# Two attentions and two FFNs on Trainium2: the last eight query groups of the second attention run behind its first steps, and its query tiles come in another order

## The reference

```python
x = x + attn_a(layernorm(x))   # differential attention, 8 heads of 2 x 64, full softmax
x = x + ffn(layernorm(x))      # one 1024 x 1024 matrix rounded to int4, bias, rank-16 LoRA
x = x + attn_b(layernorm(x))   # causal attention, 16 heads of 64, rotary q and k
x = x + ffn(layernorm(x))      # the same weights again
```

```python
q, k, v = split((x @ W_qkv))             # 16 heads of 64 each
q, k = rope(q), rope(k)
att = q @ k.T / sqrt(64) + causal mask
y = softmax(att) @ v
return y @ W_o
```

## Time and profile before

| what | value |
|---|---|
| median of 3 runs | 1709.23 us (1708.33 to 1766.12) |
| the profiled execution, its own time | 1708.93 us |
| its span on the page, slowest core | 1706.1 us (1699.2 to 1706.4 us over the cores) |
| span of core 3, whose trace is read here | 1706.4 us |
| TensorE (PE) busy | 1497.0 us, 88% |
| ScalarE (ACT) busy | 1268.7 us, 74% |
| VectorE (DVE) busy | 1047.3 us, 61% |
| GpSimd (POOL) busy | 532.5 us, 31% |
| mean granted TensorE clock, core 3 | 0.966 |

### The profile page before, as it was taken

One profiled execution on the slowest core, in us unless ns is written; L12 is line 12 of the kernel. 1 busy time (PEld: TensorE's weight loads), 2 busy tenths in 40 slices (PEclk: granted clock), 3 DMA queues, 4 the chain that ended last, 5 costly groups with the idle time before them and its releaser, 6 DMA issues.

```text
span 1706.1 us, 40220 instructions; the slowest of 8 cores (1699.2 to 1706.4 us)
## 1 busy us (share of the span) xinstructions
PE 1497.0 (88%) x13132; PEld 787.9 (46%) x13344; DVE 1047.3 (61%) x1939; ACT 1268.7 (74%) x1904; POOL 532.5 (31%) x1089
## 2 busy tenths in 40 slices
PE   3899978789999999999999998759998899989987
PEld 1344434455555555555555555324443344444443
DVE  4474468878788787888878788432625454324215
ACT  2666649899999999999999999103234688878990
POOL 3010014444444444554444444522623000001001
PEclk9899989999999999999999999879997799989989
DMA  9614031211101111111111222473005222222303
GB/s 183 120 56 110 35 77 56 82 31 32 56 19 41 41 31 51 18 44 39 32 49 45 68 31 56 78 116 81 1 1 97 40 81 69 66 72 41 101 7 77
DMA packets 131468, 99.54 MB, mean 58 GB/s; under 512 B 99891, under 2 KB 115379, under 8 KB 131270
## 3 DMA queue, kind: packets, MB, share of 16 engines
q1 hardware_dynamic: 113910, 82.10, 18.0%
q0 software_dynamic: 17360, 14.88, 6.4%
HBM read 67.79 MB, written 20.97 MB: 52 GB/s over the span
## 4 chain that ended last, share of the span: by engine, by line
PE 41%; ACT 25%; issue 12%; DVE 5%; DMA 2%; POOL 0%; ACTq 0%; DVEq 0%; SPq 0%; POOLq 0%
ACT E L175 13%; PE pL L164 10%; ACT Gt L175 7%; PE pBb L164 6%; PE pY L171 5%; ACT EB L175 4%; PE pB L164 4%; PE pS L166 4%; PE pYb L171 4%; PE pL L166 3%; PE pD L164 3%; DVE Sx L184 2%; PE pS L164 1%; DMA xn<-xn 1%; PE pY L164 1%
## 5 line engine op out<-in xcount | busy, mean ns | idle before, releaser
L184 DVE TENSOR_TENSOR Sx<-pL,Gt 128x512 f32<-128x512 f32 x768 | 503.2, 685 | 138.3 <-PE pL L963 53.9
L175 ACT ACTIVATE E<-Sx 128x1024 bf16<-128x1024 f32 (+1 forms) x512 | 433.1, 846 | 15.4 <-DVE Sx L184 14.9
L175 ACT ACTIVATE EB<-pS,cst 128x1024 bf16<-128x1024 f32 (+1 forms) x320 | 296.5, 988 | 66.6 <-PE pS L166 63.7
L171 PE MATMUL pY<-V,E 128*128 128x129 bf16 x4096 | 308.2, 221 | 23.9 <-ACT E L175 11.7
L175 ACT ACTIVATE Gt<-pD 128x512 bf16<-128x512 f32 x512 | 306.4, 598 | 24.4 <-PE pD L164 15.4
L171 PEld LDWEIGHTS pY<-V,E 128*128 128x128 bf16 x4096 | 259.7, 98 | 92.7 <-issue 40.3
L166 PE MATMUL pL<-Q,K 64*128 64x256 bf16 x1536 | 198.8, 274 | 23.8 <-ACT E L175 15.8
L164 PE MATMUL pD<-Qn,K 128*128 128x256 bf16 x1024 | 196.4, 273 | 23.1 <-ACT Gt L175 15.8
L189 POOL TENSOR_SCALAR st<-st 128x1 f32<-128x1 f32 x64 | 17.8, 278 | 502.9 <-DVE st L439 486.3
L175 ACT ACTIVATE E<-pL 128x512 bf16<-128x512 f32 x256 | 154.1, 602 | 6.0 <-PE pL L171 0.5
L166 PE MATMUL pS<-Q,K 64*128 64x512 bf16 (+3 forms) x640 | 123.4, 379 | 21.8 <-ACT EB L175 15.7
(11 more groups left out here) (165 smaller groups left out, 2167.8 us busy)
## 6 DMA issues: line engine op xcount, KB each, us to landing
x<-xN SPq DMA_DIRECT2D x32, 512.0 KB, 5.2
x<-x SPq DMA_DIRECT2D x32, 512.0 KB, 3.3
out<-x SPq DMA_DIRECT2D x16, 512.0 KB, 2.8
x<-fker SPq DMA_DIRECT2D x3, 2048.0 KB
x<-WoT SPq DMA_DIRECT2D x2, 2048.0 KB
xn<-xn SPq DMA_DIRECT2D x16, 256.0 KB, 2.1
w_k<-WkT POOLq DMA_DIRECT2D x2, 1024.0 KB, 40.7
w_v<-WvT POOLq DMA_DIRECT2D x2, 1024.0 KB, 58.2
```

The costliest lines, as they stand in the source:

```text
L171: q.add(lambda e: e.matmul(out, lhsT, rhs, start=first, stop=last, skip_group_check=True))
L175: q.add(lambda e: e.activation(out, in_, func, **kw))
L184: q.add(lambda e: e.tensor_tensor(out, a, b, op))
```

## The change

- **Query groups.** The eight Q groups of tile 2 leave stage three and become a generator `last_q`. Its first 8 matmuls (all of head pair 0) are issued ahead of the attention; the rest is the first generator of the background. It uses `pY[0]` as its only bank and `pY[1]` for the permuted product. When it ends it frees `Wo`, starts the load of `WoB` and the load of the third block of `x`.
- **No barrier.** `phase_barrier` goes. The first score waits for GpSimd's last rope addition of the first pair of tiles, the first exponential for the last matmul of stage three's groups. The PSUM banks of stages three and four are now the same tensors: `pS` are `pL`, the three Y banks are `pD`, `pB` and `pY[1]`. As `pY[1]` is in use until `last_q` is over, the first eight units use the banks 0 and 1 only; after them the three go round.
- **Order of tiles.** 1, 0, 2, then the first 256 queries of tile 3, then the last 256. A step of a half tile takes two key blocks by 256 queries (four score matmuls of 256 columns, one exponential unless it is the unit's last step, which has two). Units are 8, 4, 12, 7 and 8 steps long, 312 steps in all, and a half tile's unit needs one Y bank.
- **Background.** `after_b` takes a range of blocks (4, 4, 4, 2, 2). It is added 6 steps after the tile's last unit, and `ffn` of a block starts at the earliest 4 steps after its transpose was issued (`lag`).

The core of the diff:

```diff
-    pL = [ps(f"pL{i}", p2) for i in range(4)]
+    pS = [p2.enter_context(nc.psum_tensor(f"pL{i}", [128, 2, QT], F32)) for i in range(2)]
+    pL = [pS[i // 2][:, i % 2, :] for i in range(4)]
...
         sy.wait(a_tok, xT_free.get(slot))
+        xT_clock[b] = bg.clock + state["lag"]
...
-        while b not in xT_tok:
+        while b not in xT_tok or bg.clock < xT_clock[b]:
             yield 0
...
-        for t in reversed(two):
+        for t in reversed(two) if pair == 0 else two[1:]:
             for h in range(HA):
                 group_q(t, h)
-        while late:
-            late.pop(0)()
-    phase_barrier()
-    p2.close()
+        if pair == 0:
+            while late:
+                late.pop(0)()
+            rope_tok = po.done()
+            x_free[0] = x_free[1] = ve.done()
+    w3_dead = pe.done()
+
+    def last_q(t):
+        nonlocal w_bank
+        for h in range(HA):
+            i = h % 2
+            pe.wait(w_bank, w_tok[h // 4], xs_tok[t])
+            for c in range(NCH):
+                mm(pe, pY[0][:, :], Wo[:, c, 128 * h:128 * (h + 1)], xs[t][:, c, :],
+                   c == 0, c == NCH - 1)
+                yield 1
+            p_tok = pe.done()
+            yield 0
+            ac.wait(p_tok, qb_free[i])
+            act(ac, qb[i][:, :], pY[0][:, :], AF.Copy)
+            b_tok = ac.done()
+            yield 0
+            pe.wait(b_tok, pss_free[1])
+            mm(pe, pY[1][:, :], perm[:, :], qb[i][:, :], True, True)
+            qb_free[i] = pe.done()
+            ve.wait(b_tok, t_free[i], cs_tok[t])
+            tt(ve, t1[i][:, :], pY[0][:, :], x[:, t, 0:QT], OP.mult)
+            w_bank = ve.done()
+            ve.wait(qb_free[i])
+            tt(ve, t2[i][:, :], pY[1][:, :], x[:, t, QT:2 * QT], OP.mult)
+            pss_free[1] = ve.done()
+            po.wait(pss_free[1])
+            tt(po, Q[:, h, QT * t:QT * (t + 1)], t1[i][:, :], t2[i][:, :], OP.add)
+            t_free[i] = po.done()
+            yield 0
...
+        po.wait(p_tok)
+        for hf in range(2):
+            state["WoB"] = sl_w[0].start(po, Wo[:, :, 512 * hf:512 * (hf + 1)],
+                                         w_cols(di["WoB"], 512 * hf, 512))
...
+    w_bank = pss_free[0]
+    pair1_q = last_q(2)
+    for _ in range(NCH):
+        next(pair1_q)
+    while late:
+        late.pop(0)()
...
-    pYb = [ps(f"pYb{i}", p4) for i in range(3)]
+    y_banks = [pD, pB, pY[1]]
+    ac.wait(w3_dead)
+    state["lag"] = 4
+    groups = [(QT, QT), (0, QT), (2 * QT, QT), (3 * QT, QA), (3 * QT + QA, QA)]
...
+            for p in range(last + 1):
+                steps.append((q0, nq, c, len(bank_of), [n * p + k for k in range(n)], p == last))
...
+        pe.wait(E_tok.get(s - 2), rope_tok if s == 0 else None)
+        if s < 2:
+            pe.wait(*pqk_free[2 * s:2 * s + 2])
+        if q0 == 2 * QT:
+            pe.wait(state["rope"])
...
     def y_bank(i, k):
-        return (2 * i + k) % 3
+        return k if i < HB // 2 else (bank_of[i] + k) % 3
...
         if c == HB // 2 - 1:
-            bg.add(after_b(t, [yn_tok[v] for v in range(i - c, i + 1)]))
+            toks = [yn_tok[v] for v in range(i - c, i + 1)]
+            bg.later(6, lambda: bg.add(after_b(q0, nq, toks)))
+
+    bg.gens.append(pair1_q)
```

More of the change, by code:

```diff
@@ L929, in build_program @@
     state["ln3"] = True
+    state["lag"] = 0
+    xT_clock = {}
     bg = Background()
@@ L1293, in build_program, with after_b @@
     rb = [sb(f"rb{i}", (128, 8), F32, s4) for i in range(2)]
-    p4 = contextlib.ExitStack()
-    pS = [p4.enter_context(nc.psum_tensor(f"pS{i}", [128, 2, QT], F32)) for i in range(2)]
-    pYb = [ps(f"pYb{i}", p4) for i in range(3)]
-    pB = ps("pBb", p4)
-    state["banks"] = Banks([pB[:, :]])
+    y_banks = [pD, pB, pY[1]]
+    y_free = [x_free[0], x_free[0], None]
+    ac.wait(w3_dead)
     state["ln3"] = False
-    for hf in range(2):
-        wo_tok = sl_w[0].start(po, Wo[:, :, 512 * hf:512 * (hf + 1)],
-                               w_cols(di["WoB"], 512 * hf, 512))
+    state["lag"] = 4
     out_tok = [None] * NTB
-    x_free = [None] * 4
-    xm_free = [None] * 4
+    xm_free = [w3_dead] * 4
     xT_tok.clear()
     xT_free.clear()
-    for b in range(4):
+    groups = [(QT, QT), (0, QT), (2 * QT, QT), (3 * QT, QA), (3 * QT + QA, QA)]
+    t_order = [q0 // 128 + i for q0, nq in groups for i in range(nq // 128)]
+    for b in t_order[:2] + t_order[3:4]:
         load_x(d_x2, b)
[L1312 to L1316, removed]
+    def after_b(q0, nq, y_toks):
+        bs = range(q0 // 128, (q0 + nq) // 128)
+        for b in bs:
+            yield from out_proj(b, y_toks, state["WoB"], False)
             layer_norm(b, ve, b % 4, lambda a_tok, b=b: turn_ln(b, b % 4, a_tok, b % 4))
-        for b in four:
+        for b in bs:
             yield from ffn(b, b % 4)
@@ L1321, in after_b, with key_blocks @@
             out_tok[b] = x_free[b % 4] = r_st.next(sy).start(sy, rows_of(d_out, b), x[:, b % 4, :])
[L1322 to L1326, removed]
-        for c in range(HB // 2):
-            for j in range(4 * t + 4):
-                blocks.append((t, c, j))
-    NB = len(blocks)
+            for v in t_order[t_order.index(b) + 4:][:1]:
+                load_x(d_x2, v)
+    steps = []
+    bank_of = []
+    n_banks = 0
+    for q0, nq in groups:
+        for c in range(HB // 2):
+            n = QT // nq
+            last = (q0 + nq) // 128 // n - 1
+            for p in range(last + 1):
+                steps.append((q0, nq, c, len(bank_of), [n * p + k for k in range(n)], p == last))
+            bank_of.append(n_banks)
+            n_banks += nq // QA
+    NB = len(steps)
     S_tok, E_tok, Y_tok, m_tok, yn_tok = {}, {}, {}, {}, {}
-    y_free = [None] * 3
-    def q_lo(t, j):
-        return max(0, 128 * j - QT * t)
+    def key_blocks(s):
+        q0, nq, _, _, js, _ = steps[s]
+        return [(jj, j, max(0, 128 * j - q0)) for jj, j in enumerate(js)]
     def stepb_S(s):
@@ L1339, in stepb_S @@
             return
[L1340 to L1346, removed]
+        q0, nq, c, _, _, _ = steps[s]
+        pe.wait(E_tok.get(s - 2), rope_tok if s == 0 else None)
[3 more added lines that the diff above has]
+            pe.wait(state["rope"])
+        for jj, j, lo in key_blocks(s):
+            for hd in range(2):
+                rows = slice(64 * hd, 64 * (hd + 1))
+                mm(pe, pS[s % 2][:, hd, nq * jj + lo:nq * (jj + 1)],
+                   K[rows, c, 128 * j:128 * (j + 1)], Q[rows, c, q0 + lo:q0 + nq], True, True,
+                   (64 * hd, 0))
         S_tok[s] = pe.done()
```

82 lines of the change are left out of this document (48 added, 34 removed).

## The result

The changed kernel takes 1700.4 us (median of 8, beside 1709.4 for the kernel before on the same chip): ratio 0.994, 95% interval 0.992 to 0.996. It is faster, by 0.6% where 1.8% was forecast. That is inside the 2% that the prediction took for hard to tell from no change, and outside its stated range of 1663 to 1695. Two further facts frame what follows.

The account below looks back on a forecast made before the run. TensorE bounds steps with background, ScalarE those without. Start 1286.9 plus stages 67.8, 36.2, 112.8, 138.2 and 34.4 gave a span of 1676.3; with 2.5 us above the span, 1679 us, range 1663 to 1695.

Parts of the forecast that it names:

- What bounds the kernel: Stage four: steps with background bound by TensorE, steps without by ScalarE; some 100 of 320 steps go without.
- C: Tile 2 of the attention, 96 steps, all with background: 112.8 us, bounds 108 to 117.
- D: Tile 3 of the attention in two halves, 120 steps: 138.2 us, bounds 131 to 143.
- Start: Attention's first exponential comes at about 1286.9, 17.3 us earlier, with seven groups, a GpSimd wait and the barrier gone.
- A: Tile 1, 64 steps, 38 with moved groups at 9.2 us a unit, 26 without background: 67.8 us, bounds 60 to 75.
- B: Tile 0, 32 steps, 4.7 us a unit with background, 3.8 without: 36.2 us, bounds 31 to 44.
- E: Drain from last exponential to end: 34.4 us where 43.6 before, with a new 6.0 us transpose wait; bounds 30 to 40.
- R2: Rival: VectorE and the Y banks become the bound in tiles 1 and 0 and the drain; 1692 us, chance 0.12.
- R3: Rival: TensorE's clock stays at 1.2 GHz through tiles 1 and 0; 1725 us, slower than before, chance 0.03.
- R1: Rival: added waits cost nothing, more slack in tiles 1, 0 and 3; 1666 us, chance 0.27.
- R4: Rival: late `WoB` load or transposes delay the background, drain as long as before; 1690 us, chance 0.04.
- The port that VectorE and GpSimd share: Beside moved groups, some 4 of 19 VectorE masks wait 0.6 us on GpSimd additions: 2.6 us, mostly hidden.

Follow-up runs that it names:

- shift2: Changed kernel with the first background generator after tile 1 started two attention steps later; ratio 0.986 to the kernel before.
- shift1: Changed kernel with the first background generator after tile 1 started one attention step later; ratio 0.983 to the kernel before.
- hold: Changed kernel with the first background generator after the moved groups held back 32 steps more, so tile 0 runs without background; one execution took 1710.4 us.
- tile0_first: Changed kernel with tile 0 first and tile 1 second, background after the moved groups still starting near step 70; ratio 0.990 to the kernel before.
- groups_stage3: shift2 with the eight query groups back in stage three, all units using three Y banks in turn; ratio 0.989 to the kernel before.

## Why the prediction was wrong, point by point

**What bounds the kernel: right.** Steps with background are TensorE's, steps without are ScalarE's as long as the clock is up. The prices taken from unit starts held within 3%: C and D came to 250.1 us for 251.0 forecast, with another number of steps and another order. That the sum is so close is luck in part, since C was 3.1 us short and D 2.1 long.

**Start: right.** Forecast 1286.9; 1284.2 to 1286.5 on seven cores, 1286.5 on shift2's slowest. Core 7's 1291.8 comes from a lateness that the change did not make.

**A: right in size on core 7, with luck.** 68.6 for 67.8. The wait for the second Y bank, priced at 0.3 us a unit, hardly shows (0.3 us in all of the groups' stretch). A unit took 9.24 us in shift2 ((1332.70 - 1286.49) / 5) all the same, for 9.2 forecast, though the last two of these 40 steps have no groups. The clock was not at 1.00 from the first exponential, as forecast: in the first unit it was 0.82 or 0.83 on four cores, which took 9.5 to 9.9 us for it, and 0.69 on the four others, which took 11.1 or 11.2. It was 1.00 in the next four units on every core. On five cores one or more of the three units without groups ran at 0.50, where such a unit takes 8.3 us for 7.1 at 1.00. So A was 72.1 to 72.4 us on four cores, a cost that the sum did not have; it did not decide the time only because core 7, which ended last, was not among them.

**B: the step that failed.** I wrote: "I take 4.7, times 6.5 units = 30.5", from 8.93 less four full steps, with VectorE as "the near bound". In place of 4.7 a unit took 7.0, and the stage 53.0 for 36.2. As a price of the work alone the 36.2 was sound (37.8 in shift1, 36.6 in shift2), though partly by luck: the two first units, without projections, took 4.7 and 4.2 us for 3.8, the six others 4.6 on average for 4.7, and shift2 has 24 steps of background in tile 0 where the sum had 26. What the sum had no term for was where in a unit the background's waits fall, and what the fallen clock behind such a wait adds. I had treated 8.93 as a mean price. It is one phase too: a unit of tile 1 has 8 steps and so has `out_proj`, and three units in a row, from 1351.46 on, took 8.93 us each. It was a phase in which TensorE stood 0.36 us for the add. The sign of it stood in the trace of before, core 3, where TensorE waits inside that unit for the residual add in the single bank:

```profile
1357.99 0.81 PE L164 MATMUL pBb<-Wo,Q 128*128 128x512 bf16 x3 [0.36 <-DVE x L184]
```

I counted it as part of a price instead of asking what stands behind it when the unit's end stands before it. My upper bound for B (44) was worked out as more work per unit, so it did not hold the 53.0 either.

**E: the right chain, 3.7 us short.** The new wait was 6.09 us for 6.0 (of which the prices given in the prediction make 5.3; aggregate and what follows it have none there). Missing were the waits for the single bank before the drain gets its four others (1.05 and 1.01 us) and half of the price of the fallen clock (1.5 forecast; 16 matmuls and the small ones took about 2.9 more).

**Rivals.** R2 had the place (tile 0, VectorE's end of unit) but as load: 5.5 us a unit and VectorE as the bound. VectorE was busy 20.91 of 42.10 us in the changed kernel. The cause is order, not load. R3 had the clock as a cause that stays down from the start through A and B: the groups' stretch ran at 0.96 on core 7. In B it was 0.74, and about 1.4 of the 7.0 us of a unit go to it, as said above; hold, with nothing behind tile 0, was faster at 0.54. So R3 was right for a part of B, but not as the cause that starts it: one step of delay gave the clock back. R1 did not occur in A, D or B. R4 did not occur: the two halves of `WoB` were issued at 1340.3 and 1341.3, landed 14.5 us later (median), and the first projection came at 1369.2 without a wait for them.

**The port that VectorE and GpSimd share.** The changed kernel has the case that no row of before had. Masks on VectorE in the stretch of the moved groups, then in the rest of the attention (duration in ns: min, median, max):

```profile
L184 DVE TENSOR_TENSOR EB<-EB,c_tri x18: 280/292/1262, 1297.6 to 1337.3; 128x256 bf16<-128x256 bf16 x18
```

```profile
L184 DVE TENSOR_TENSOR EB<-EB,c_tri x62: 281/292/294, 1425.5 to 1655.0; 128x256 bf16<-128x256 bf16 x62
```

Two of the 18 waited, one for 1262 ns in place of 292 and one for 479, beside these additions:

```profile
1309.76 1.38 POOL L184 TENSOR_TENSOR Q<-ro 128x512 bf16<-128x512 f32 x1 [4.96 <-DVE ro L184]
...
1310.81 0.48 DVE L184 TENSOR_TENSOR EB<-EB,c_tri 128x256 bf16<-128x256 bf16 x1 [0.80 <-ACT EB L175]
...
1326.93 1.27 POOL L184 TENSOR_TENSOR Q<-ro 128x512 bf16<-128x512 f32 x1 [4.13 <-DVE ro L184]
...
1327.08 1.78 DVE L184 TENSOR_TENSOR EB<-EB,c_tri 128x256 bf16<-128x256 bf16 x3 [0.30 <-ACT EB L175]
```

Both masks began while the addition beside them ran, and ended 0.15 us after it did (the row at 1327.08 merges three masks, of which the first is the long one). By the Trainium skill, SBUF — State Buffer, section "SBUF: two separate sides", the one that starts later is blocked until the other's whole instruction is over; the trace agrees, in two cases of 18 for the four estimated, 1.2 us in sum for 2.6. It is the same two masks on every core. tile0_first has more: 6 of the 30 masks beside its moved groups waited (418 to 1144 ns), 2.8 us in sum, on its slowest core.

## What to carry to other kernels

When work is threaded behind a loop in fixed pieces, write down both periods. If one divides the other, every wait of the background recurs at the same place of the loop, and a price per step taken from another loop is the price of one phase of it; shift the start by a step or two and time each phase, it is one number. And ask of each background wait what stands behind it in the same in-order queue: here a score that nothing but the queue's order tied to a residual add. In a drain, look for the piece that waits for nothing and put it behind the last producer of a long chain, not ahead of it.

## What was not expected of the hardware

Tile 1 without the groups ran at a granted clock of 0.55 for 63 us on the slowest core of groups_stage3, though TensorE's row was busy 93% of it (59.01 of 63.30) and never idle for more than 0.45 us at once after its first unit; tile 0 alone ran at 0.54 with the row busy 77%. A busy row was thus no sign here that the clock was up. Nor is it the same on every core: in the same window and execution the eight cores had 0.53 to 0.83. With matmuls of 512 columns of the moved groups between the steps, the second to the fourth unit of tile 1 had 1.00 on all of them.

Where TensorE is just behind ScalarE in need, the level decides which of them sets the pace: a unit of eight steps without background takes 7.14 us at 1.00 (1338.48 to 1345.62 in the changed kernel, core 7) and 8.28 at 0.50 (the seventh unit of tile 1 on core 0 of the same execution).
